# Self attention: heads of Q and K put into their rows by transfers through scratch memory, in place of selector products and their evictions

## The reference, cut to what matters

```
hn = _layernorm(x, ln1_g, ln1_b)                          # 4 x 512 x 128
q = (hn @ wq + bq).reshape(b, s, 16, 8).transpose(0, 2, 1, 3)
k = (hn @ wk + bk).reshape(b, s, 16, 8).transpose(0, 2, 1, 3)
v = (hn @ wv + bv).reshape(b, s, 16, 8).transpose(0, 2, 1, 3)
scores = einsum('bhqd,bhkd->bhqk', q, k) / sqrt(8)        # 16 heads, 512 x 512 each
attn = softmax(scores)
o = einsum('bhqk,bhkd->bhqd', attn, v) ... @ wo + bo
```

## Time and profile before

| what | value |
|---|---|
| runs | 1109.92, 1114.28, 1120.05 us (median 1114.28) |
| span of the profiled execution, first to last instruction | 1110.5 us |
| its own time | not given beside the span; the span lies within the spread of the runs |
| instructions | 15394 |
| TensorE busy | 905.3 us (82%), 5738 matmuls |
| VectorE busy | 607.6 us (55%) |
| ScalarE busy | 437.0 us (39%) |
| mean granted TensorE clock | 0.889 of full speed |
| the self attention stage, first raw score to last exponential | 739.8 to about 1013 us |

### The profile page before, as it was taken

The page is one execution under the profiler, slowest core; times in us unless marked ns, Lnnn a source line. Parts: engine busy times, 40 slices in busy tenths (PEclk is TensorE's granted clock), DMA queues, the critical chain, the costliest instruction groups (busy, mean ns, idle before and its releaser), DMA issues.

```text
span 1110.5 us, 15394 instructions
## 1 busy us (share of the span) xinstructions
PE 905.3 (82%) x5738; PEld 492.8 (44%) x5738; DVE 607.6 (55%) x1629; ACT 437.0 (39%) x750; POOL 225.0 (20%) x226
## 2 busy tenths in 40 slices
PE   4788866987768786496898899868889889887988
PEld 2334544654424443375465334323334334344766
DVE  4455664445554534343733454557777777773644
ACT  2344323332333222110331333335767667665333
POOL 1100050434161211234321100100000000200354
PEclk9799897998977867598789799987999999999899
DMA  9900011232137000311001000000000000102030
GB/s 284 304 23 1 1 35 47 70 95 63 45 111 231 26 22 30 89 35 49 19 1 45 1 2 1 1 1 1 1 1 1 2 1 2 40 1 73 29 106 15
DMA packets 43248, 52.87 MB, mean 48 GB/s; under 512 B 6078, under 2 KB 32830, under 8 KB 42488
## 3 DMA queue, kind: packets, MB, share of 16 engines
q1 hardware_dynamic: 37864, 42.61, 12.6%
q0 software_dynamic: 5312, 9.29, 2.6%
HBM read 37.45 MB, written 23.26 MB: 55 GB/s over the span
## 4 chain that ended last, share of the span: by engine, by line
PE 58%; DVE 19%; issue 9%; ACT 5%; DMA 4%; POOL 4%; SPq 1%; POOLq 0%; DVEq 0%; ACTq 0%
PE PS L182 50%; DVE KB L2022 5%; DVE KB L1624 2%; PE PS L659 2%; POOL RB L2323 1%; DVE Ht L1538 1%; POOL d L2313 1%; PE PS L1136 1%; DVE st L1525 1%; DVE ON L1691 1%; DMA RB<-d 1%; ACT KB L1432 1%; POOL dbuf L2243 1%; POOL ve L2216 1%; DVE OT L1666 1%
## 5 line engine op out<-in xcount | busy, mean ns | idle before, releaser
L2022 DVE TENSOR_REDUCE KB<-PS 128x2 fp32r<-128x1024 f32 x128 | 154.5, 1221 | 47.3 <-PE PS L182 46.2
L1286 ACT ACTIVATE PT<-PS 77x512 f32<-77x512 f32 x192 | 98.1, 590 | 169.8 <-PE PS L182 169.8
L182 PE MATMUL PS<-CX 32*77 32x512 f32 (+2 forms) x896 | 125.5, 570 | 18.1 <-DVE OT L1666 6.8
L2216 POOL TENSOR_TENSOR ve<-ve,nh 128x4 f32<-128x4 f32 x40 | 41.7, 1042 | 446.0 <-DVE ve L1533 445.8
L1624 DVE TENSOR_REDUCE KB<-PS 128x16 fp32r<-128x1232 f32 x48 | 69.1, 1440 | 75.0 <-PE PS L182 75.0
L182 PE MATMUL PS<-RA,RB 128*128 x152 | 85.3, 645 | 8.7 <-issue 3.9
L1452 ACT ACTIVATE PT<-PS 128x1024 f32<-128x1024 f32 x74 | 75.6, 1023 | 35.6 <-PE PS L182 34.6
L182 PE MATMUL PS<-QB,KB 64*128 64x512 f32 x256 | 59.1, 459 | 20.9 <-DVE KB L2022 18.5
L182 PEld LDWEIGHTS PS<-CX 32*128 32x128 f32 (+1 forms) x896 | 48.6, 191 | 61.9 <-issue 16.6
L182 PE MATMUL PS<-KB,QB 64*128 64x512 f32 x256 | 65.7, 514 | 5.3 <-DVE KB L2022 3.2
L182 PE MATMUL PS<-PT,VB 77*32 77x512 f32 x384 | 56.6, 664 | 8.0 <-DVE KB L1624 6.3
(11 more groups left out here) (318 smaller groups left out, 1626.7 us busy)
## 6 DMA issues: line engine op xcount, KB each, us to landing
d<-d SPq DMA_DIRECT2D x2, 1472.0 KB, 10.0
dbuf<-in_c_fill SPq DMA_DIRECT2D x1, 2580.0 KB, 20.2
RB<-d SPq DMA_DIRECT2D x10, 256.0 KB, 3.1
o<-CX SPq DMA_DIRECT2D x10, 256.0 KB, 2.5
RA<-in_l_w SPq DMA_DIRECT2D x1, 2304.0 KB, 10.3
RB<-d SPq DMA_DIRECT2D x4, 514.0 KB, 4.4
d<-OT SPq DMA_DIRECT2D x2, 1024.0 KB, 6.7
RB<-in_l_w SPq DMA_DIRECT2D x1, 2048.0 KB, 11.1
```

What stands on the lines that cost most here:

```text
L182: return e.matmul(o, l, r, start=first, stop=last, skip_group_check=True)
L1286: e.activation(slot[s][0:NK, :], PS[0:NK, 4 + j, :], ACT.Exp, bias=0.0, scale=a.scale).then_inc(*expd(i, r, j))
L2022: e.tensor_reduce(o, PS[:, k:k + 2, :], AX, ALU.max).then_inc(*rmax("s", s, t, p2))
L2216: e.tensor_tensor(ve[:, 8 * par + 4:8 * par + 8], ve[:, 8 * par:8 * par + 4], nh[:, :], ALU.pow).then_inc(*rstd(*key))
```

## The change

`first` issues nothing any more on TensorE, ScalarE and VectorE; its place in the round is one, 0.4. SyncE gets two new streams. `self_norms` writes the four operands of a batch (upper and lower part of Q and K) to scratch tensors `zqk` in device memory, in six transfers of 256 KB, three for Q and three for K: each head has 32 rows of 512 there, and the upper part goes to two of its planes of 8 rows. `first` then reads a group's rows: one transfer of 256 KB for Q and four of 64 KB for K, one for each head. Rows 24 to 31 of each head in scratch are filled at the hook `l3x1` by eight transfers of 256 KB from a constant, c_z, in place of the load and the cast of the selectors. GpSimd zeroes the three KS pairs once. `second` waits for the transfers (`placed`) in place of the evictions, the eviction of a batch's Q and K two batches later waits for the writes, and two buffers of the experts are now free when `fourth(11)` is done.

```diff
-        SELm = RR[:, 6144:8192].rearrange("p (k g n) -> p k g n", k=4, g=4)
+        PLANES = [((0, 2), (1,)), ((0, 1), (2,))]
 # TensorE
             def first(s):
-                b, g = s // 4, s % 4
-                w.wait_ge(*pinit.at("sel"))
-                for n, (N, done) in enumerate(((QN[b % 2], qact), (KNv[b % 2], kact))):
-                    k, free = banks.take(done, "s", s)
-                    w.wait_ge(*free)
-                    w.wait_ge(*qsplit.at("n", b, n))
-                    mm(e, PS[:, k, :], SELm[:, 2 * n, g, :], N[0], True, False)
-                    mm(e, PS[:, k, :], SELm[:, 2 * n + 1, g, :], N[1], False, True).then_inc(*(kproj if n else projected)("s", s))
-                    yield from idle(3 if n else 2)
+                yield
             def second(s):
-                w.wait_ge(*qact.at("s", s))
-                w.wait_ge(*kact.at("s", s))
+                w.wait_ge(*placed[s % 3].at("s", s))
 # ScalarE, self_norms
-                        w.wait_ge(*(kproj if n else projected).at("s", 4 * b - 5))
+                        w.wait_ge(*zw[b - 2].all())
 # ScalarE
             def first(s):
                 yield
-                w.wait_ge(*projected.at("s", s))
-                w.wait_ge(*qs_free(s))
-                e.activation(QS[s % 3], PS[:, banks.of(qact, "s", s), :], ACT.Copy).then_inc(*qact("s", s))
-                yield from idle(2)
-                w.wait_ge(*kproj.at("s", s))
-                w.wait_ge(*ks_free(s))
-                for n in range(2):
-                    e.activation(KS[s % 3][n], PS[:, banks.of(kact, "s", s), :], ACT.Identity, bias=msk[:, 44 + n:45 + n],
-                                 scale=msk[:, 42 + n:43 + n]).then_inc(*kact("s", s))
-                    yield
 # GpSimd, hook
-                if name == "l3x1":
-                    w.wait_ge(*ld["l3sel"].all())
-                    e.tensor_copy(RR[:, 6144:8192], RB[:, 6144:8192]).then_inc(*pinit("sel"))
+                if name == "self":
+                    w.wait_ge(*scored.at(23, 3, 3))
+                    for n in range(3):
+                        e.memset(KB[:, 1024 * n:1024 * n + 1024].bitcast(F32), 0.0).then_inc(*pinit("ks", n))
 # SyncE
+            def self_norms(b):
+                yield from idle(13)
+                for n, N in enumerate((QN[b % 2], KNv[b % 2])):
+                    Z = zqk[n][b].rearrange("(a r) c -> a r c", r=32)
+                    for lo in range(2):
+                        w.wait_ge(*(qsplit if lo else qact).at("n", b, n))
+                        for p in PLANES[n][lo]:
+                            e.dma_start(Z[:, 8 * p:8 * p + 8, :], N[lo].bitcast(F32)).then_inc(*zw[b](n, p))
+
+            def first(s):
+                b, g = s // 4, s % 4
+                w.wait_ge(*zw[b].all())
+                w.wait_ge(*ld["zc"].all())
+                w.wait_ge(*qs_free(s))
+                e.dma_start(QS[s % 3].bitcast(F32), zqk[0][b][128 * g:128 * g + 128, :]).then_inc(*placed[s % 3]("s", s))
+                w.wait_ge(*ks_free(s))
+                w.wait_ge(*pinit.at("ks", s % 3))
+                for j in range(4):
+                    e.dma_start(KS[s % 3][j % 2][32 * j:32 * j + 32, :].bitcast(F32),
+                                zqk[1][b][128 * g + 32 * j:128 * g + 32 * j + 32, :]).then_inc(*placed[s % 3]("s", s))
+                yield
 # SyncE, hook l3x1
-                    w.wait_ge(*pe2.at(19, "down"))
-                    load("l3sel", RB[:, 6144:8192], A["l3_sel"])
+                    for b in range(NB):
+                        for n in range(2):
+                            load("zc", zqk[n][b].rearrange("(a r) c -> a r c", r=32)[:, 24:32, :], A["c_z"][n])
 # buffers of the experts
-            return ... if q >= 2 else kproj.at("s", 15)
+            return ... if q >= 2 else weighed.at("s", 11, 3)
-            return (weighed.at("s", 11, 3), kproj.at("s", 15), ...)[q]
+            return (weighed.at("s", 11, 3), weighed.at("s", 11, 3), ...)[q]
 # order
-                    streams.append((first(i), [0.31, 0.345, 0.43, 0.475, 0.6]))
+                    streams.append((first(i), [0.4]))
```

More of the change, by code:

```diff
@@ L192, in program @@
         KB = sb("KB", 3 * 2048, F32R)
-        with nc.sbuf_tensor("RR", [128, 8192], F32R) as RRt:
-            RR = RRt
         RB = sb("RB", 8192)
@@ L240, in program @@
         dbuf = nc.dram_tensor("dbuf", (8 * CAP, ROW1), F32, kind="Internal").ap()
+        zqk = [[nc.dram_tensor(f"z{n}{b}", (512, 512), F32, kind="Internal").ap() for b in range(NB)] for n in "qk"]
         x1 = nc.dram_tensor("x1", (NB * S, 128), F32, kind="Internal").ap()
@@ L388, in program @@
               ("l0", "l0b", "ctx", "c", "x0", "x1", "x2", "x3", "c2", "rb", "cb", "l0f", "l1", "l2", "zero", "zero3",
-               "l1f", "l2w", "l3x", "l3f", "l1b", "l3s", "l3sel", "l2m", "c3", "c0", "zero0")}
+               "l1f", "l2w", "l3x", "l3f", "l1b", "l3s", "zc", "l2m", "c3", "c0", "zero0")}
         mq = [signal("mq0", 16), signal("mq1", 16)]
+        zw = [signal(f"zw{b}", 16) for b in range(NB)]
+        placed = [signal(f"placed{n}", 16) for n in range(3)]
         sc1 = [signal(f"sc1{b}", 16) for b in range(NB)]
@@ L2012, in first @@
             def first(s):
-                yield from idle(5)
+                yield
             def second(s):
@@ L2516, in sync @@
             load("zero", dbuf.rearrange("(p t) d -> p (t d)", p=128), A["c_fill"])
-            order(nothing, nothing, front, nothing, nothing, nothing, route, capacity, nothing, nothing, nothing, nothing, maxima, nothing, nothing,
+            order(nothing, nothing, front, nothing, nothing, nothing, route, capacity, nothing, self_norms, first, nothing, maxima, nothing, nothing,
                   nothing, nothing, nothing, experts3, nothing, nothing, nothing, experts0, nothing, hook)
@@ L2527, in x3_free @@
         def x3_free(q):
-            return e3.at("u", tiles3.index((q - 2, quads3[q - 2][2] - 1))) if q >= 2 else kproj.at("s", 15)
+            return e3.at("u", tiles3.index((q - 2, quads3[q - 2][2] - 1))) if q >= 2 else weighed.at("s", 11, 3)
         def raw3_free(q):
@@ L2534, in raw3_free @@
                 return resid.at("o", q - 4)
-            return (weighed.at("s", 11, 3), kproj.at("s", 15), scored.at("s", 15, 3, 1), scored.at("s", 15, 3, 1))[q]
+            return (weighed.at("s", 11, 3), weighed.at("s", 11, 3), scored.at("s", 15, 3, 1), scored.at("s", 15, 3, 1))[q]
         def o3_free(q):
@@ L2758 @@
         msk[:, 44 + n] = -1.0 * (part == 24) * msk[:, 42 + n]
-    sel = _np.zeros((4, 4, 128, 128), _np.float32)
-    for g in range(4):
-        for j in range(4):
-            for k, places in enumerate(((0, 2), (1,), (0, 1), (2,))):
-                for n in places:
-                    for d in range(8):
-                        sel[k, g, 32 * g + 8 * j + d, 32 * j + 8 * n + d] = 1.0
+    rows_z = _np.zeros((2, 16, 8, 512), _np.float32)
+    rows_z[1, :, 0] = -1.0
     place8 = _np.arange(128).reshape(4, 4, 8).transpose(1, 0, 2).ravel()
@@ L2818 @@
                                   I["L3_xattn_Wproj"][place8]], 1),
-        "l3s_w": _np.concatenate([I["L3_ffn_wq"], I["L3_ffn_wk"], I["L3_ffn_wv"], I["L3_ffn_wo"]], 1), "l3_sel": sel.transpose(2, 0, 1, 3).reshape(128, 2048),
+        "l3s_w": _np.concatenate([I["L3_ffn_wq"], I["L3_ffn_wk"], I["L3_ffn_wv"], I["L3_ffn_wo"]], 1), "c_z": rows_z,
         "l3_w1": I["L3_ffn_w1"], "l3_w2": I["L3_ffn_w2"],
```

## The result

| | before | after |
|---|---|---|
| median of the runs | 1112.25 us (1109.92 to 1120.05, 4 runs) | 1097.64 us (1096.14 to 1098.80, 4 runs) |
| span of the profiled execution | 1110.5 | 1094.4 |
| mean granted TensorE clock | 0.889 | 0.884 |

The ratio is 0.9856, interval 0.9813 to 0.9898. A second measurement, on another chip, gave 0.9838 (0.9789 to 0.9887; 1097.18 against 1112.77). The change makes the kernel 1.4 to 1.6% faster. The forecast was 1096 us and 18.0 us off the span; the span lost 16.1, the medians differ by 14.6.

The account below looks back on a forecast made before the run. TensorE was taken to lead, VectorE to follow. 3.4 + 1.1 + 1.3 + 7.9 + 4.8 + 1.0 - 1.5 = 18.0 us off, put against the median 1114.28: 1096 us, its own range 1088 to 1103, the whole range 1082 to 1110.

Parts of the forecast that it names:

- The bound: Whole stage: no engine is full, but on the whole TensorE leads and VectorE follows, having waited 46.2 us for TensorE.
- The start, 3.4 us: Stage start: first raw scores need only the transfers and come at 736.3 instead of 739.76, a gain of 3.4 us.
- Round 1, 0: Round 1: VectorE holds it, busy 20.1 of 24 us, so removing its selectors is worth nothing.
- Rounds 2 and 3, 2.4 us: Round 2, at half clock: K's selector pair worth 1.1 us; round 3: both pairs worth 1.3 us.
- K pair 7.9: Rounds 4 to 15: removing K's two selector matmuls saves 0.66 us in each of 12 rounds, 7.9 us.
- Q pair 4.8: Rounds 4 to 15: removing Q's two selector matmuls saves 0 to 0.6 us a round, limited by maxima transfers; 4.8 us.
- Evictions 1.0: ScalarE's evictions: on the chain in five rounds, each worth the 0.20 us wait for bank 6; 1.0 us.
- Late transfers, -1.5: Rounds 3, 7 and 11: reads behind the six writes come late, a loss of 0.5 us each, 1.5 us.
- 1 (other waits take the place): VectorE, bank pairs and maxima transfers hold the rounds instead: only 9 us off, 1105; chance 0.16.
- 2: Rounds 2 and on: TensorE idles more and its clock stays low, some 7.5 us per slow round; chance 0.06.
- 3 (late transfers): Reads 3 us late in rounds 4, 8 and 12, no gain at the start: 7 us off, 1107; chance 0.10.
- 4 (all on the chain counts): All 25 selector pairs on the chain and the evictions count in full: 28 us off, 1086; chance 0.08.

Follow-up runs that it names:

- one transfer: Changed kernel with the four transfers of a group's maxima made one: 1092.92 us, against 1097.18 of the changed kernel on that chip.
- Q alone: Kernel before with only Q moved to transfers, K still by selector products and evictions: 1109.61 us, ratio 0.9985 to the kernel before.
- K alone: Kernel before with only K moved to transfers, Q still by selector products and eviction: 1100.73 us, ratio 0.9886 to the kernel before.
- e_start_only: Kernel before with only the first group by transfers, the fifteen others by selectors and evictions: 1110.16 against 1112.73 us, ratio 0.9967.

## Why the prediction was right, and where not

**The bound.** Right: TensorE's own work led. Its products put back take 4.15 of 5.07 us away, and VectorE's wait for it fell by 14.8 us.

**The start, 3.4 us.** Right: 3.39 from the last output product to the first transposition, 3.49 to the first raw scores. The cover was forecast at half a us and was 2.8: in the median 256 KB landed in 2.7 us and 64 KB in 2.5, not in the 3.6 of the earlier trace rows, and the reads could start 2.4 us after the last write's issue. GpSimd's three fills took 2.73 us, less than the 3.7 taken for them. The gain is capped by TensorE's arrival.

**Round 1, 0.** Right: the first raw scores came 3.94 us earlier (739.76 to 735.82) and the first maxima 3.84.

**Rounds 2 and 3, 2.4 us.** Wrong: they grew by 0.07. In round 2 the K pair was not the bound. TensorE's timeline after, at half clock:

```profile
752.38 0.80 PE L182 MATMUL PS<-QB,KB 64*128 64x512 f32 x2 [2.42 <-DMA QB<-KB]
...
755.93 0.80 PE L182 MATMUL PS<-QB,KB 64*128 64x512 f32 x2 [0.84 <-DVE KB L2004]
...
760.88 2.05 PE L182 MATMUL PS<-S,HT 128*128 128x128 f32 x8
```

The maxima's transfer and then VectorE took its place, and products ran at the lower level until about 762.8, 14.8 us into the round, where before they left it 13.8 us in. The other execution, with 17.80 us and a clock of 0.67 in round 2 against 0.62, says that the length of this round is the clock's first. In round 3 1.0 of the 1.3 us were there (13.04 with one transfer, 14.06 before) and the late read of K took 0.9 of them.

**Rounds 4 to 15, K pair 7.9 and Q pair 4.8.** By kind of round the sum was forecast at 0.96, 1.26 and 1.26 us for rounds 6, 7 and 8; measured 0.97, 1.27 and 0.29. So the fault is one: rounds 8 and 12 have no more than 0.3 to give, because VectorE waited only 0.19 us for TensorE beside the pairs. The working had taken VectorE's room as a mean (12.8 of 17 us), and put these rounds among the six in which Q counts in full; its other support, that 25 of 26 pairs lie on the chain of waits, tells that a pair was on the longest path but not how close the next path was. The split was off too: Q alone gave 0.78 in six rounds where 3.0 was forecast, and only 0.4 of it, in rounds 7 and 11, is clear of what two traces with the same work differ by. It paid 1.44 once K's pair was gone as well, since VectorE's waits beside both pairs go only when both are gone (round 6: 0.87 us before, 0.69 with Q moved, 0.64 with K moved, none with both). K alone, with its evictions, gave 3.63 against 4.0.

**Evictions 1.0.** Right in size and kind: 0.26 us in each of rounds 7 and 11, where a product had waited 0.20 us for K's eviction, and 0.29 us of ScalarE's time in six rounds; at most 0.9 in all. Whether the three other rounds in which the forecast counted 0.2 gave it is not shown.

**Late transfers, -1.5.** Too much, and not in three places: 0.8 to 0.9 us, all in round 3, where the round is shortest (14 us against 17.6); rounds 7 and 11 showed no such wait. There the last of K's reads was issued at 834.37 and 897.76 and landed 2.8 and 2.9 us later, 2.1 and 1.9 us ahead of the first raw scores. Of the working's two legs, all transfers together 3.6 us beyond their issues (12.5 us into the round) and one behind the other at 1024 KB in 6.7 us (17.0), the first held: the last read landed 13.0 us into round 7. Behind the six writes the read of 256 KB took 4.0 to 4.3 us instead of 2.7, so they slowed it by some 1.5 us, not by the 10 us of their data.

**The total.** Rounds 4 to 15 gave 12.40 us against 12.2, closer than the steps deserve. The dip of round 9 (17.81 us at a clock of 0.90 before, 15.48 at 1.00 after) is in it. Taking for each round the shorter of two traces with the same work in it (before and e_start_only, 196.1; after and its second execution, 185.0) the gain is 11.1. What rounds 8 and 12 and 2 and 3 fell short of was made up in part by the smaller loss to transfers and by that dip. The absolute number had luck too: 18.0 us were taken off 1114.28, the median of three runs, and with a fourth run the median before is 1112.25. The forecast of 1096 lies 1.6 us from the 1097.64 measured, the forecast gain 3.4 us from the 14.6 between the medians.

**Rivals.** 1 (other waits take the place) holds in rounds 2, 8 and 12 and for Q alone, and nowhere else. 2: the granted clock was 0.97 in rounds 5 to 15 both before and after, with 20.0 us of TensorE's idle time in them before and 23.7 after. So the oscillation that the Trainium skill ("TensorE: Matmul & The Clock Gate", A second HAM failure mode: psum-queue depth-cycling) warns of did not grow with the idle time here. 3 (late transfers): in one round of three. 4 (all on the chain counts): not in rounds 8 and 12, where VectorE waited 0.19 us beside two pairs of 0.66.

## What to carry to other kernels

Price a removed instruction in each kind of round by itself, by how long the next engine waited for this one beside it: here the sums of VectorE's waits that went (0.87, 1.34 and 0.19 us) gave the gain within some 0.2 us in both traces of before, while VectorE's busy time in a round (13.3 us in two kinds that gained 0.97 and 0.29) said nothing. The waits before alone are an upper bound: in round 7 2.23 us stood there and 0.89 stayed. Removing work from the leading engine and moving it to idle transfers is worth up to that second bound, and pieces removed together can be worth more than alone. Before adding transfers to a queue, look at the shortest round that they must fit in and at the small issues that stand ahead of them: with 1.9 us of those off the queue, the wait for the late read was gone.

## What was not expected of the hardware

The granted clock dips for part of a round in different rounds of two executions of the same kernel, and one dip costs 1 to 2.4 us. The changed kernel's round 9 (columns as for rounds 7 and 8), then rounds 9 and 12 of its other execution:

```profile
856.23:871.72 15.49, 13.11 (x118) 5.99 (x114) 13.28 (x27) 9.53 (x12) 1.01 (x1) 1.00 0.13 35
```

```profile
853.10:869.64 16.54, 14.31 (x118) 6.12 (x114) 13.32 (x27) 9.52 (x12) 1.01 (x1) 0.90 0.12 33
901.76:919.90 18.14, 16.08 (x122) 7.79 (x118) 14.12 (x33) 9.76 (x12) 2.30 (x2) 0.81 0.10 31
```

The same instructions took 15.49 us at a clock of 1.00 and 16.54 at 0.90, and round 12 took 18.14 at 0.81 against 15.74. Such a dip is at least as large as what the change gives in most rounds, so single rounds of two traces are compared only at the same clock.
